# A graph layer with attention over edges, one core: the value product one step later, GpSimd waiting on ScalarE's counts, three PSUM banks each in the first phase, the scatters after the last record gather

## The chip, the core and the metric

One core of one Trainium2 chip runs the whole program. The metric is the device time of one execution in microseconds (us), lower is better. Below, PE is TensorE, DVE is VectorE, ACT is ScalarE, POOL is GpSimd and SP is SyncE.

## The reference

There are 100,000 nodes with 128 features each and 25,000 edges with a sender `snd` and a receiver `rcv`; the kernel sorts them by receiver. In the kernel's words:

```
score = silu(silu([x[rcv], x[snd], attr3, weight1] @ W1 + b1) @ W2 + b2) @ W3 + b3     one number an edge
alpha = softmax of score over the edges of one receiver
out[rcv] += alpha * node_vec[snd] * (x[snd] @ Wv)
result = layernorm(x + (x + out)) over the 128 features, all 100,000 rows
```

So every row of x is normalized at least as it is (the dense part), and the rows of receivers are written a second time with their sum (the edge part).

## The kernel before

**Groups and blocks.** The edges are padded to G = 49 groups of 512 (four tiles of 128). The dense part is 49 blocks of 2048 rows: SP loads a block (L306), DVE takes its statistics (L905, eight instructions), ACT and DVE normalize it in place (L477, 13 rows of 16; L920, the other three), SP stores it (L314). `dense_plan()` gives each block a turn: 17 of them in the first phase, one in three turns, the rest from the first step of the second phase on, eight in nine steps.

**First phase, 52 turns.** For each group in the senders' order: POOL gathers the sender's rows into the record ring (`hs`, L415, four indirect DMAs a group), PE transposes them (L583, bank i % 2), ACT copies the transpose to SBUF (L487, `hsT`, a ring of two), PE multiplies by the sender's part of W1 and adds the product of the edge attributes (L576 and L577, bank 2 + j % 4), ACT copies this into the record (L492), and SP writes the record to DRAM (L344). DVE sorts the edges by receiver meanwhile. PE's order in a turn i is: products of group i - 2, then the transposes of group i.

**Second phase, 66 steps.** It goes through the groups in the receivers' order. A group passes through these instructions, in the steps named (s is the step, g the group):

- POOL: gather of the receivers' rows (`hk`, L415, ten groups ahead), gather of the records (`r`, L415, ring of 12 groups), both four indirect DMAs a group
- PE, step g - 1: transposes of the receivers' rows (L596, `turn_rows`); ACT, step g: their copy (L500)
- PE, step g + 1: first layer, the product (L629) and the record added by four transposes (L631), which give `mm1_done`; ACT: first Silu (L510, `x1_ready`)
- PE, step g + 2: second layer (L623, `mm2_done`); ACT: second Silu (L505, `x2_ready`)
- PE, step g + 3: score (L616). Every four groups make a batch; DVE takes the batch's softmax in two parts (L943 to L953 and L959 to L964) with ACT's Exp (L515) between them
- PE, step g + 9: the receivers' numbers spread along rows (L606, `krow_ready`); DVE: the weight matrix (L973, `weights(g)`, `m_ready`)
- PE, step g + 10: the weighted sum of senders' rows (L645, `z_ready`); ACT: its copy `zs` (L520, `zs_ready`); PE, at the end of the same step: the product with Wv (L654, `y_ready`)
- DVE, step g + 11: the sum with the receiver's row (L982, `rows(g)`, `y_done`) and its statistics (L987); ACT, five steps or more later: the normalization (L529, `res_ready`)
- POOL: scatter of the finished rows to the output (`sc`, L419, four indirect DMAs a group)

All engines run in the order in which their instructions are written; the waits are on counts. PE's order in a step is: L606 (first waiting for `m_ready` of the group before, since bank 4 is reused), L616, L623, L629 and L631, a small transpose every fourth step (L639), L645, L596, L654. DVE's order in a step is: L920 of the dense block, `rows(s - 11)`, every fourth step the first part of the softmax, the dense statistics L905, `weights(s - 9)`, the second part of the softmax; the short instructions that turn statistics into factors (L876 to L890) are put between them.

**POOL's order** is written by `pool_plan()`: all `hs`; ten `hk`; then `r` and `hk` in turn; when the `hk` are used up, `r` 39 to 48 and `sc` 0 to 9 in turn (`SC_FROM` works out to 39); then the scatters 10 to 48. What POOL waits for before a group: `hs` g for T_ready (PE's transposes of group g - 5), `hk` 0 to 9 for A_ready (PE's products), `r` g for mm2_done (PE's second layer of group g - 3) and z_ready (group g - 12), `sc` g from 8 on for z_ready of group g + 26 and each for res_ready. After the last scatter POOL issues two more small scatters (L423), for receivers whose edges span tiles.

## Time and profile before

| what | us |
|---|---|
| median of 3 runs, lowest, highest | 1186.98, 1179.71, 1191.53 |
| the profiled execution | 1186.11 |
| its span, first to last instruction | 1177.9 |
| POOL busy | 752.8 (64%) |
| PE, DVE, ACT busy | 635.3, 586.4, 523.2 |

The span is 8.2 us shorter than the profiled execution's own time, and that one is 0.9 us under the median. Busy time of POOL is the writing of descriptors for indirect DMAs, 784 of them for the groups in four kinds (186.5, 189.9, 185.5 and 188.7 us); the 0.30 us between two of them counts as idle.

### The profile page before, as it was taken

To read this page: it belongs to the slowest core of one execution; us is meant where nothing else is said; L and a number is where in the kernel's file an instruction comes from. 1 tells how busy PE (TensorE), PEld (TensorE's weight loads), DVE (VectorE), ACT (ScalarE), POOL (GpSimd) and SP (SyncE) were. 2 spreads that over 40 slices of the span, in tenths; PEclk is the share of its full clock that TensorE was granted. 3 is DMA by queue.
4 is the path that set the end of the run, shared out by engine and by line. 5 is a ranking of instruction groups with operands and counts; after the bars stand their busy time and mean duration, and the time that the engine had idled before them with its cause. 6 is when DMAs were issued, how large, how long until landed. Compare 5 with 4: busy or idle time off the path is not lost.

```text
span 1177.9 us, 11360 instructions
## 1 busy us (share of the span) xinstructions
PE 635.3 (54%) x2783; PEld 436.6 (37%) x2783; DVE 586.4 (50%) x2276; ACT 523.2 (44%) x1168; POOL 752.8 (64%) x790
## 2 busy tenths in 40 slices
PE   2388778869703445666755766665555636610000
PEld 1256555546401222444434544444344425610000
DVE  4587665564431544597657766853323135532000
ACT  0255354355522556567667858765334324340000
POOL 7566666666677565656646656664656665577775
PEclk9999999999999976787877777787778777655555
DMA  6388877879974486575747566742212211121111
GB/s 207 101 257 289 256 261 245 275 263 253 292 240 147 162 287 235 165 249 188 243 159 242 200 214 213 245 143 81 72 55 68 68 54 40 44 71 52 53 51 38
DMA packets 77913, 199.67 MB, mean 170 GB/s; under 512 B 18999, under 2 KB 49398, under 8 KB 65304
## 3 DMA queue, kind: packets, MB, share of 16 engines
q1 hardware_dynamic: 49560, 134.47, 32.0%
q0 software_dynamic: 28288, 64.48, 20.4%
q8 instruction: 23, 0.38, 0.1%
q14 instruction: 42, 0.34, 0.1%
HBM read 106.74 MB, written 92.26 MB: 169 GB/s over the span
## 4 chain that ended last, share of the span: by engine, by line
PE 22%; ACT 21%; issue 18%; another core or an unknown queue 18%; POOL 10%; DVE 7%; SPq 2%; DMA 2%; ACTq 0%; POOLq 0%; DVEq 0%
ACT xin L477 12%; POOL out_rows L419 10%; PE bank L576 8%; PE bank L583 3%; ACT hk L529 3%; PE bank L577 3%; PE bank L654 2%; DVE dst L905 2%; PE bank L616 2%; PE bank L623 1%; DMA xin<-in_x 1%; ACT x L510 1%; ACT zs L520 1%; ACT hkT L500 1%
## 5 line engine op out<-in xcount | busy, mean ns | idle before, releaser
L415 POOL DMA_INDIRECT region<-rec_d,id_t x196 | 186.5, 952 | 172.4 <-PE bank L623 53.0
L477 ACT ACTIVATE xin<-xin,drs 128x128 f32<-128x128 f32 x637 | 257.9, 484 | 52.9 <-issue 32.4
L415 POOL DMA_INDIRECT hk<-in_xw,snd_t x196 | 189.9, 969 | 102.6 <-issue 54.9
L419 POOL DMA_INDIRECT out_rows<-hk,sidx_t x196 | 188.7, 963 | 76.4 <-issue 57.8
L415 POOL DMA_INDIRECT hk<-in_x,kg_t x196 | 185.5, 946 | 66.1 <-issue 58.8
L654 PE MATMUL bank<-wvh,zs 128*128 128x128 f32 x392 | 86.5, 389 | 215.6 <-ACT zs L520 151.3
L576 PE MATMUL bank<-w1b,region 128*128 128x128 f32 x392 | 151.3, 489 | 66.3 <-issue 43.7
L905 DVE BATCH_NORM_STATS2 dst<-xin 128x6 f32<-128x256 f32 x392 | 137.6, 416 | 67.1 <-DMA xin<-in_x 50.1
L654 PEld LDWEIGHTS bank<-wvh,zs 128*128 128x128 f32 x392 | 73.4, 280 | 227.2 <-ACT zs L520 159.3
L576 PEld LDWEIGHTS bank<-w1b,region 128*128 128x128 f32 x392 | 99.1, 313 | 91.8 <-issue 56.0
L982 DVE TENSOR_TENSOR hk<-bank,hk 128x512 f32<-128x512 f32 x49 | 33.8, 689 | 185.0 <-PE bank L654 79.4
L616 PE MATMUL bank<-x,wz 128*16 128x128 f32 x392 | 79.3, 372 | 26.7 <-ACT x L505 15.9
L505 ACT ACTIVATE x<-bank,bcol 128x512 f32<-128x512 f32 x49 | 33.6, 686 | 129.4 <-remote 105.9
L487 ACT ACTIVATE region<-bank 128x512 f32<-128x512 f32 x49 | 28.9, 590 | 138.9 <-PE bank L583 61.3
L623 PE MATMUL bank<-x,w2s 128*128 128x512 f32 x98 | 72.0, 824 | 19.9 <-ACT x L510 19.3
L529 ACT ACTIVATE hk<-hk,ers 128x128 f32<-128x128 f32 x196 | 79.8, 483 | 4.6 <-issue 3.2
L973 DVE TENSOR_SCALAR m_q<-bank,kcol,acol 128x128 f32<-128x128 f32 x196 | 73.4, 403 | 2.4 <-remote 2.2
L629 PE MATMUL bank<-hkT,w1a 128*128 128x512 f32 x98 | 55.2, 647 | 20.3 <-DMA region<-rec_d,id_t 19.4
L616 PEld LDWEIGHTS bank<-x,wz 128*16 128x16 f32 x392 | 45.6, 127 | 50.2 <-issue 18.8
L583 PE MATMUL bank<-ident,hk 128*128 128x128 f32 x196 | 54.3, 432 | 16.0 <-DMA w<-hk 16.0
L645 PE MATMUL bank<-m_q,region 128*128 128x128 f32 x392 | 59.3, 297 | 1.7 <-issue 1.6
L510 ACT ACTIVATE x<-bank,bcol 128x512 f32<-128x512 f32 x49 | 33.2, 677 | 57.3 <-remote 34.7
(179 smaller groups left out, 913.0 us busy)
## 6 DMA issues: line engine op xcount, KB each, us to landing
xin<-in_x SPq DMA_DIRECT2D x49, 1024.0 KB
out_rows<-xin SPq DMA_DIRECT2D x49, 1024.0 KB
rec_d<-hk SPq DMA_DIRECT2D x49, 514.0 KB
hk<-in_xw,snd_t POOLq DMA_INDIRECT x196
hk<-in_x,kg_t POOLq DMA_INDIRECT x196
region<-rec_d,id_t POOLq DMA_INDIRECT x196
out_rows<-hk,sidx_t POOLq DMA_INDIRECT x196
ef_d<-hk SPq DMA_DIRECT2D x9, 196.0 KB
```

Source lines behind the costliest of these rows:

```text
L415: pool.indirect_dma_start(out=to, out_offset=None, in_=frm, in_offset=bass.IndirectOffsetOnAxis(ap=index, axis=0)).then_inc(done, 16)
L419: pool.indirect_dma_start(out=out, out_offset=bass.IndirectOffsetOnAxis(ap=index, axis=0), in_=frm, in_offset=None).then_inc(done, 16)
L477: ins = nc.scalar.activation(xin[:, j % X_RING, n, :], xin[:, j % X_RING, n, :], ACT.Identity, bias=drs[:, j % 2, 1, n:n + 1], scale=drs[: ...
L529: ins = nc.scalar.activation(hk[:, g, q, :], hk[:, g, q, :], ACT.Identity, scale=ers[:, b % 2, 0, n:n + 1], bias=ers[:, b % 2, 1, n:n + 1])
L576: pe.matmul(to, hsT[:, j % 2, q * P:(q + 1) * P], w1b[:], start=True, stop=False)
L583: ins = pe.transpose(bank[i % 2][:, q * P:(q + 1) * P], rec[:, i % HS_RING, q, H:2 * H], ident[:])
L616: ins = pe.matmul(bank[3][0:BT, 0:P], wz[:, BT - 1 - n:2 * BT - 1 - n], x2[:, q * P:(q + 1) * P], start=(n == 0), stop=(last and q == TPG ...
L623: pe.matmul(bank[2][:], w2s[:], x1[:], start=True, stop=True).then_inc(S["mm2_done"], 1)
L645: ins = pe.matmul(bank[5][:, q * P:(q + 1) * P], rr[:, g % R_RING, q, H:2 * H], m_q[:, g % 2, q, :], start=True, stop=True)
L654: ins = pe.matmul(bank[6][:, q * P:(q + 1) * P], zs[:, q * P:(q + 1) * P], wvh[:], start=True, stop=True)
L905: ins = vec.bn_stats(dst[:, n:n + 2, :].rearrange("p j w -> p (j w)"), xin[:, j % X_RING, n:n + 2, :].rearrange("p j h -> p h j"))
L973: ins = vec.tensor_scalar(m_q[:, g % 2, q, :], bank[4][:, q * P:(q + 1) * P], kcol[:, t:t + 1], acol[:, b % 2, n:n + 1], ALU.is_equal, ALU ...
```

## The change

1. PE's product with Wv (L654 before) leaves the end of step g + 10 and stands in step g + 11, behind the first layer's L631 and ahead of L639 and L645. DVE's `rows(g)` stays in step g + 11.
2. POOL waits for ACT's counts where it waited for PE's: `hsT_ready` for T_ready (one group further ahead), `rec_ready` for A_ready (one further ahead), `x2_ready` for mm2_done (distance unchanged), `zs_ready` for z_ready ahead of the scatters. The wait of `r` for z_ready, which frees the ring, stays.
3. In the first phase the transposes use three banks, their copies a ring of three, and the products three banks instead of four; the waits follow these numbers.
4. No scatter stands between the record gathers: `sc` 0 comes after `r` 48.

```
+HST_RING, T_BANKS, A_BANKS = 3, (0, 1, 5), (2, 3, 4)
-HS_AHEAD, HK_AHEAD, R_AHEAD = 5, 6, 3
+HS_AHEAD, HK_AHEAD, R_AHEAD = 6, 7, 3
...
-        elif sc < G and r >= min(SC_FROM, G):
+        elif sc < G and r == G:
...
-                    wait(pool, "T_ready", g - HS_AHEAD + 1)
+                    wait(pool, "hsT_ready", g - HS_AHEAD + 1)
...
-                        wait(pool, "A_ready", min(G, G - HK_AHEAD + g))
+                        wait(pool, "rec_ready", min(G, G - HK_AHEAD + g))
...
-                    wait(pool, "mm2_done", g - R_AHEAD + 1)
+                    wait(pool, "x2_ready", g - R_AHEAD + 1)
...
-                        wait(pool, "z_ready", min(G, g + SC_AHEAD))
+                        wait(pool, "zs_ready", min(G, g + SC_AHEAD))
...
-                    wait(act, "A_ready", j - 1)
-                    nc.scalar.activation(hsT[:, j % 2, :], bank[j % 2][:], ACT.Copy).then_inc(S["hsT_ready"], 1)
+                    wait(act, "A_ready", j - HST_RING + 1)
+                    nc.scalar.activation(hsT[:, j % HST_RING, :], bank[T_BANKS[j % 3]][:], ACT.Copy).then_inc(S["hsT_ready"], 1)
...
-                    wait(pe, "rec_ready", j - 3)
+                    wait(pe, "rec_ready", j - 2)
...
-                    wait(pe, "hsT_ready", i - 1)
+                    wait(pe, "hsT_ready", i - 2)
...
+                g = s - Z_LAG - 1
+                if 0 <= g < G:
+                    wait(pe, "zs_ready", g + 1)
+                    wait(pe, "y_done", g)
+                    for q in range(TPG):
+                        ins = pe.matmul(bank[6][:, q * P:(q + 1) * P], zs[:, q * P:(q + 1) * P], wvh[:], start=True, stop=True)
+                    ins.then_inc(S["y_ready"], 1)
...
-                if 0 <= g < G:
-                    wait(pe, "zs_ready", g + 1)
-                    wait(pe, "y_done", g)
-                    for q in range(TPG):
-                        ins = pe.matmul(bank[6][:, q * P:(q + 1) * P], zs[:, q * P:(q + 1) * P], wvh[:], start=True, stop=True)
-                    ins.then_inc(S["y_ready"], 1)
```

PE in a middle step of the second phase, before, from one second-layer product (L623) to the next step's L616:

```order
L623 MATMUL bank<-x,w2s 128x512 [waits x2_ready,x1_ready]
L629 MATMUL bank<-hkT,w1a 128x512 [waits x1_ready,r_in10,hkT_ready]
L631 MATMUL bank<-ident,region 128x128 x4
L645 MATMUL bank<-m_q,region 128x128 [waits zs_ready,m_ready]
L645 MATMUL bank<-m_q,region 128x128 x3
L596 MATMUL bank<-ident,hk 128x128 [waits hkT_ready,hk_in4]
L596 MATMUL bank<-ident,hk 128x128 x3
L654 MATMUL bank<-wvh,zs 128x128 [waits y_done,zs_ready]
L654 MATMUL bank<-wvh,zs 128x128 x3
L606 MATMUL bank<-ident,kcol 128x128 [waits m_ready]
L606 MATMUL bank<-ident,kcol 128x128 x3
```

The same place after the change (the lines are two lower up to the new place, L650 is the old L645, L637 the old L654):

```order
L621 MATMUL bank<-x,w2s 128x512 [waits x2_ready,x1_ready]
L627 MATMUL bank<-hkT,w1a 128x512 [waits x1_ready,r_in10,hkT_ready]
L629 MATMUL bank<-ident,region 128x128 x4
L637 MATMUL bank<-wvh,zs 128x128 [waits y_done,zs_ready]
L637 MATMUL bank<-wvh,zs 128x128 x3
L650 MATMUL bank<-m_q,region 128x128 [waits zs_ready,m_ready]
L650 MATMUL bank<-m_q,region 128x128 x3
L594 MATMUL bank<-ident,hk 128x128 [waits hkT_ready,hk_in4]
L594 MATMUL bank<-ident,hk 128x128 x3
L604 MATMUL bank<-ident,kcol 128x128 [waits m_ready]
L604 MATMUL bank<-ident,kcol 128x128 x3
```

The product with Wv no longer follows its own zs; it stands ahead of L650, with the group before.

POOL around the last record gathers, before (`region` is the record ring, `sidx_t` the rows to write):

```order
L419 DMA out_rows<-hk,sidx_t 125089x128 [waits res_ready,dense_written]
L419 DMA out_rows<-hk,sidx_t 125089x128 x3
L415 DMA region<-rec_d,id_t 128x257 [waits mm2_done,z_ready]
L415 DMA region<-rec_d,id_t 128x257 x3
L419 DMA out_rows<-hk,sidx_t 125089x128 [waits res_ready]
L419 DMA out_rows<-hk,sidx_t 125089x128 x3
L415 DMA region<-rec_d,id_t 128x257 [waits mm2_done,z_ready]
```

After the change, around the last record gather:

```order
L413 DMA region<-rec_d,id_t 128x257 [waits x2_ready,z_ready]
L413 DMA region<-rec_d,id_t 128x257 x3
L417 DMA out_rows<-hk,sidx_t 125089x128 [waits res_ready,dense_written]
L417 DMA out_rows<-hk,sidx_t 125089x128 x3
L417 DMA out_rows<-hk,sidx_t 125089x128 [waits res_ready]
L417 DMA out_rows<-hk,sidx_t 125089x128 x3
```

Ten scatter groups, 40 indirect DMAs, have moved from between the last ten record gathers to behind them.

## Rows read from the trace of the kernel before

**Rows 1.** Windows: second phase with dense blocks, without, last scatters; times in us

```profile
core 0: us, PE busy (x) PEld busy (x) DVE busy (x) ACT busy (x) POOL busy (x), PEclk, DMA share, GB/s
492.00:833.00 341.00, 214.76 (x1090) 151.34 (x1088) 230.53 (x885) 228.78 (x513) 204.83 (x216) 0.77 0.58 193
833.00:945.00 112.00, 66.18 (x362) 47.30 (x362) 34.35 (x109) 41.93 (x80) 70.03 (x73) 0.77 0.22 64
1042.00:1169.00 127.00, 1.60 (x6) 0.86 (x6) 13.82 (x56) 9.64 (x23) 96.46 (x101) 0.50 0.18 57
```

**Rows 2.** Timeline, POOL, steps 23 and 24: start us, length us, instruction [idle before]

```profile
644.62 0.94 POOL L415 DMA_INDIRECT region<-rec_d,id_t  x1 [2.38 <-PE bank L645]
...
649.61 0.94 POOL L415 DMA_INDIRECT hk<-in_x,kg_t  x1 [0.30 <-issue]
...
653.36 0.94 POOL L415 DMA_INDIRECT hk<-in_x,kg_t  x1 [0.30 <-issue]
656.90 0.94 POOL L415 DMA_INDIRECT region<-rec_d,id_t  x1 [2.60 <-PE bank L623]
```

**Rows 3.** Timeline, PE, one step of the second phase, at the lower clock

```profile
635.07 2.07 PE L654 MATMUL bank<-wvh,zs 128*128 128x128 f32 x8 [4.11 <-ACT zs L520]
636.94 0.63 PE L606 MATMUL bank<-ident,kcol 128*128 128x128 bf16 x4
637.50 1.89 PE L616 MATMUL bank<-x,wz 128*16 128x128 f32 x8
639.32 1.85 PE L623 MATMUL bank<-x,w2s 128*128 128x512 f32 x2
641.01 1.02 PE L629 MATMUL bank<-hkT,w1a 128*128 128x512 f32 x2
641.87 0.60 PE L631 MATMUL bank<-ident,region 128*128 128x128 f32 x4
642.31 1.06 PE L645 MATMUL bank<-m_q,region 128*128 128x128 f32 x8
643.20 0.60 PE L596 MATMUL bank<-ident,hk 128*128 128x128 f32 x4
```

**Rows 4.** Timeline, ACT, the same step

```profile
643.88 0.69 ACT L505 ACTIVATE x<-bank,bcol 128x512 f32<-128x512 f32 x1 [3.39 <-remote]
...
646.70 1.28 ACT L515 ACT_TABLE_LOAD   x1
...
648.21 0.57 ACT L520 ACTIVATE zs<-bank 128x512 f32<-128x512 f32 x1
```

**Rows 5.** Timeline, DVE, from rows (L982) to the weights (L973), three steps

```profile
637.18 0.69 DVE L982 TENSOR_TENSOR hk<-bank,hk 128x512 f32<-128x512 f32 x1 [3.49 <-PE bank L654]
...
645.54 0.41 DVE L973 TENSOR_SCALAR m_q<-bank,kcol,acol 128x128 f32<-128x128 f32 x1
...
652.82 0.69 DVE L982 TENSOR_TENSOR hk<-bank,hk 128x512 f32<-128x512 f32 x1
...
658.03 0.41 DVE L973 TENSOR_SCALAR m_q<-bank,kcol,acol 128x128 f32<-128x128 f32 x1
...
856.07 0.69 DVE L982 TENSOR_TENSOR hk<-bank,hk 128x512 f32<-128x512 f32 x1 [8.38 <-remote]
...
857.47 1.35 DVE L973 TENSOR_SCALAR m_q<-bank,kcol,acol 128x128 f32<-128x128 f32 x4
```

**Rows 6.** Timeline, POOL: first phase, every third group of sender gathers

```profile
184.47 0.94 POOL L415 DMA_INDIRECT hk<-in_xw,snd_t  x1 [2.81 <-PE bank L583]
...
202.03 0.94 POOL L415 DMA_INDIRECT hk<-in_xw,snd_t  x1 [2.84 <-PE bank L583]
```

**Rows 7.** Timeline, POOL: record gather 39, record gather 48, a stall, last group scatter

```profile
833.17 0.94 POOL L415 DMA_INDIRECT region<-rec_d,id_t  x1 [2.73 <-PE bank L645]
...
944.55 0.99 POOL L415 DMA_INDIRECT region<-rec_d,id_t  x1 [3.73 <-PE bank L645]
...
973.21 0.95 POOL L419 DMA_INDIRECT out_rows<-hk,sidx_t  x1 [3.67 <-remote]
...
1167.57 0.95 POOL L419 DMA_INDIRECT out_rows<-hk,sidx_t  x1 [0.30 <-issue]
```

More of the change, by code:

```diff
@@ L89 @@
 DSTEP = dense_plan()
-SC_FROM = DSTEP[-1] - B0 + 5
 def pool_plan():
@@ L182, in part @@
             return region[:, at[0] - size:at[0]]
-        hsT = part(2 * GE).rearrange("p (r e) -> p r e", r=2)
+        hsT = part(HST_RING * GE).rearrange("p (r e) -> p r e", r=HST_RING)
         ef = part(EF_RING * GE // 2).bitcast(BF16).rearrange("p (r e) -> p r e", r=EF_RING)
@@ L491, in _ @@
                     wait(act, "A_ready", j + 1)
-                    nc.scalar.activation(rec[:, j % HS_RING, :, 0:H], bank[2 + j % 4][:].rearrange("p (q h) -> p q h", q=TPG), ACT.Copy
+                    nc.scalar.activation(rec[:, j % HS_RING, :, 0:H], bank[A_BANKS[j % 3]][:].rearrange("p (q h) -> p q h", q=TPG), ACT.Copy
                                          ).then_inc(S["rec_ready"], 1)
@@ L572, in _ @@
                     wait_ring(pe, ef_in, j, 16)
-                    wait(pe, "rec_ready", j - 3)
+                    wait(pe, "rec_ready", j - 2)
                     for q in range(TPG):
-                        to = bank[2 + j % 4][:, q * P:(q + 1) * P]
-                        pe.matmul(to, hsT[:, j % 2, q * P:(q + 1) * P], w1b[:], start=True, stop=False)
+                        to = bank[A_BANKS[j % 3]][:, q * P:(q + 1) * P]
+                        pe.matmul(to, hsT[:, j % HST_RING, q * P:(q + 1) * P], w1b[:], start=True, stop=False)
                         ins = pe.matmul(to, ef[0:36, j % EF_RING, q * P:(q + 1) * P], w36[:], start=False, stop=True)
@@ L580, in _ @@
                     wait_ring(pe, hs_in, i, 16 * TPG)
-                    wait(pe, "hsT_ready", i - 1)
+                    wait(pe, "hsT_ready", i - 2)
                     for q in range(TPG):
-                        ins = pe.transpose(bank[i % 2][:, q * P:(q + 1) * P], rec[:, i % HS_RING, q, H:2 * H], ident[:])
+                        ins = pe.transpose(bank[T_BANKS[i % 3]][:, q * P:(q + 1) * P], rec[:, i % HS_RING, q, H:2 * H], ident[:])
                     ins.then_inc(S["T_ready"], 1)
```

## The prediction

> **What bounds the kernel now.** I read the busy shares first: no engine is near full, POOL is highest at 64%. So I cut the span into stages (windows) and looked in each for the engine whose instructions stand in a row with the same gap at the same place.
>
> At the end it is POOL. The last scatter starts at 1167.57 and nothing but the two small ones and the landing comes after it: 1168.5 to 1177.9, 9.4 us [rows 7]. Between 1042 and 1169 us POOL issues 101 indirect DMAs in 127 us, 1.26 us each, of which 0.96 is work and 0.30 the step to the next [rows 1]; that is 5.05 us a group of four, and no wait is left there. So the end is the moment at which POOL may begin its uninterrupted scatters plus their number times 5.05 us. Record gather 48 is issued at 944.55 and takes 5.05, so it is done at 949.6; 39 scatter groups follow up to 1168.5, 218.9 us, against 39 x 5.05 = 197.0 without a stall. 22 us are waits for the last sums, one of which is seen ending at 973.21 [rows 7].
>
> In the middle, 492 to 833 us, there is a step of 12.2 to 12.3 us. POOL shows it: a record gather at 644.62, eight indirect DMAs until 654.30, idle for 2.60 us, the next record gather at 656.90 [rows 2]; 10.0 of work and 2.3 of waiting for PE's count. PE shows its own loop: the Wv product waits 4.11 us for ACT's zs [rows 3], and behind it come L606, L616, L623, whose result ACT's second Silu reads, and after more of ACT's work the next zs at 648.21 [rows 4]. Both loops have the same length, so either may lead. One thing counts for what follows: by its row L623 ends at 641.17, yet ACT and POOL, both waiting for it, start at 643.88 and 644.62 [rows 2 to 4]. PE's counts arrive up to 2.7 us behind the ends in its rows, and there POOL had gone idle (at 642.24) shortly before. The Trainium skill, "Perfetto Trace Analysis", section "Tensor Engine Instruction (MATMUL, LD_WEIGHTS)", says that TensorE's end is an estimate from the size and that the count follows the acknowledgement of PSUM; it gives no size for the delay. The trace agrees that there is one.
>
> In the first phase POOL issues three sender groups, 15.0 us, and then waits 2.84 us: 17.56 us from 184.47 to 202.03, 5.85 us a group [rows 6].
>
> **The change, part by part, against the profiled execution (span 1177.9 us, 8.2 us around it, 0.9 us below the median).**
>
> *First phase: 0 us, bounds -33 and +10.* POOL's wait for T_ready of group g - 5 becomes one for the copy of group g - 6. The copy follows its transposes at once or, where ACT is in a block of 13 norms, behind that block; the extra group ahead is 5 us of POOL. I let them cancel. The third bank for the transposes frees nothing by itself: in PE's order the products of group i - 2, which wait for that group's copy, stand ahead of the transposes of group i, so the old wait was already met. If the gap of 2.5 us went in each third group of 39, it would be 13 x 2.5 = -33; if each became 0.7 longer, +10. I take 0: the loop of copy, products and transposes between PE and ACT is untouched.
>
> *Second phase, record gathers wait for x2_ready: +0.7 us a step.* The group is the same, so the wait can only end later, by one Silu, 0.69 us [rows 4]; in the step behind an Exp also by a table load, 1.28 us [rows 4]. POOL's loop becomes 12.3 + 0.7 = 13.0 us, every fourth step 14.3. Behind the waiting gather stand the four gathers of receivers' rows, ten groups ahead, which nobody lacks.
>
> *Wv product a step later: the zs wait goes, and a tighter loop comes.* The 4.11 us wait of PE [rows 3] is gone, since zs of the group before is long there. What is late next is m_ready. Before, DVE's rows(g) used a product made a step earlier; now the product of group g is made in the same step g + 11, in the middle of PE's list. DVE does rows, statistics and the weights in this order, and L606 at the head of PE's next step waits for these weights. So each step has the loop: L606 to the Wv product on PE, rows to weights on DVE. PE's part at the lower clock: 636.94 to 642.31 for L606 to L631, 5.4 us, plus 2.07 for the product, 7.5 us [rows 3]. DVE's part: 652.82 to 658.44, 5.6 us; in the fourth step with the softmax 637.18 to 645.95, 8.8 us [rows 5]. With 0.1 for the handing over: 13.2 us, and 16.4 in every fourth step. The granted clock of the stage is 0.77 [rows 1], that is about half the time at 2.4 instead of 1.2 GHz, which takes some 2 us off PE's part in such steps; then POOL's 13.0 leads. Four steps together: 13.1, 13.1, 14.3 and 15.0, mean 13.9 against 12.2. That is +1.7; I take +1.6: the stage's 27 steps have 341 us, 12.6 each [rows 1], so some are longer than 12.3 by other causes and should absorb theirs. Bounds: 0 a step (DVE's part finds room that I don't see) and +2.8 (all at the lower clock and PE's counts late as well).
> Steps 12 to 38, 27 of them: 27 x 1.6 = +43 us. Steps 3 to 11 have only the x2 part: 9 x 0.7 = +6 us.
>
> *Record gathers 39 to 48 without scatters between them: -20 us.* Now nine steps take 944.55 - 833.17 = 111.4 us, 12.4 each [rows 7], though there is no dense block left and POOL has 10 us of work in each. Then POOL has 5 us, and the PE and DVE loop leads: DVE's part is 856.07 to 858.82, 2.8 us [rows 5], PE's at most 7.5, so 10.3 us, one in four longer by the softmax, some shorter at the higher clock. I take 10.2: 9 x 2.2 = 20. Bounds: 0 and -40 (8 us a step, the clock at 2.4 GHz).
>
> *Scatters: ten groups move to the end.* What stands after gather 48 is 49 x 5.05 = 247.5 us instead of 197.0, +50.5 us, on the path in full. The 22 us of waits in that stretch were waits for sums of the last groups; twelve groups that need none of them now come first, so most is covered. I keep 5, bounds 0 and 25. zs_ready for z_ready adds 0.6 us at a hold and is within this.
> The Trainium skill, "Perfetto Trace Analysis", section "Optimization Strategy", says that where the most-contended engine changes over time, interleaving the regimes may help. This part undoes such an interleaving. By the rule alone the price is the 50.5 us; by the rows the scatters were not free where they stood, and 20 come back.
>
> *Sum.* Gather 48 is issued at 944.6 + 0 + 6 + 43 - 20 = 973.6; + 5.05 + 247.5 + 5 + 9.4 = 1240.5 us of span; + 8.2 + 0.9 = 1249.6. I round to 1249 us, 5% more than 1187.
>
> **The rivals.**
> *Only the scatters count.* The new loop costs nothing, POOL's Silu wait is hidden, the last nine steps give 20: gather 48 at 924.6, span 1191.5, time 1201 us. For it: DVE has only 230.5 us of work in the 341 of the stage [rows 1]. Against it: the order is fixed, and DVE idles for the product, not for lack of work. Chance 0.20, half of it within 1% of now.
> *Faster: POOL's gap closes.* With the zs wait gone PE's second layer could be done while POOL is still issuing, so that gather g never waits: a step is POOL's 10.0 us. 27 x 2.3 = 62 us and 20 in the last steps put gather 48 at 862.6, span 1129.5, time 1139 us. It needs m_ready to come early, which rows 5 speak against. It decides from where gather 48 is issued before 917: 917 + 5.05 + 247.5 + 9.4 is today's 1178 of span. Chance 0.12.
> *Slower still: late counts on top.* PE's counts are late while POOL issues without a pause (the 3.67 us stall at 973.21 follows 25 us of such issuing [rows 7]), and now DVE's rows wait for one of them in the middle of the step. A step of 15.0 in steps 12 to 38 gives 27 x 2.8 = 76, ten more in the first phase, 20 more of holds: 1249 + 33 + 10 + 20 = 1312 us at the end, 1290 as its middle. Chance 0.16.
>
> **How the numbers follow.** The forecast has 0.52. The likeliest alone spans 1225 to 1275 (step +0.8 to +2.6 and the holds). For 8 in 10 the range goes down to the scatters-only case and up into the late-counts one: 1195 to 1292. About 1% is what a measurement of this kernel tells from no change. Slower by over 1%: 0.52 + 0.16 + 0.10 from the scatters-only case + 0.01 = 0.79. Within 1%: 0.08 of that case. Faster: 0.12, and 0.01 of rest.
>
> **What would show it.** In the timeline of the changed kernel: PE no longer waits for ACT's zs, and its first L604 of a step waits for DVE's m_q; DVE's L982 waits for the Wv product in each step and L973 ends some 5.6 us later; POOL's gap before a record gather is 3 us or more, released by ACT; gather 48 between 950 and 1000; then 49 scatter groups of 5.05 us with almost no gap. I am wrong if the steps between 492 us and the end of the dense blocks stay at 12.3 us or less, if gather 48 comes before 925, or if the scatters don't end the program.

## The result, and the profile after

The changed kernel takes 1274.06 us (median of 4 runs, 1270.66 to 1278.11) beside 1187.75 us (4 runs) for the kernel before: 1.077 times as long, 95% interval 1.072 to 1.082. The forecast was 1249 with a range of 1195 to 1292. The profiled execution of the changed kernel took 1270.66 us, its span 1262.5.

The same stages as in [rows 1], cut where the changed kernel has them (record gathers 12 to 38, 39 to 47, then two pieces of the scatters):

```profile
core 0: us, PE busy (x) PEld busy (x) DVE busy (x) ACT busy (x) POOL busy (x), PEclk, DMA share, GB/s
501.00:899.00 398.00, 219.79 (x1087) 141.92 (x1087) 227.12 (x876) 228.76 (x509) 204.12 (x216) 0.73 0.50 168
899.00:974.00 75.00, 58.69 (x342) 39.77 (x343) 34.70 (x113) 40.53 (x77) 33.98 (x36) 0.89 0.24 65
979.00:1122.00 143.00, 56.62 (x277) 44.63 (x277) 44.24 (x143) 30.83 (x68) 88.55 (x94) 0.62 0.13 44
1128.00:1253.00 125.00, 1.60 (x6) 0.86 (x6) 12.34 (x49) 7.88 (x19) 95.09 (x99) 0.50 0.18 57
```

Every engine does the work that it did, in a longer stage: VectorE 227 us where it had 231, ScalarE the same 229, GpSimd the same 204. The time is waiting. By the starts of the record gathers and the end of the span the 84.6 us of more span lie so:

| stretch | before | after | difference | the prediction had |
|---|---|---|---|---|
| start to record gather 0 | 349.6 | 356.8 | +7 | 0 |
| record gathers 0 to 12 | 142.6 | 144.1 | +1.5 | +6 |
| 12 to 39 | 341 | 398 | +57 | +43 |
| 39 to 48 | 111.4 | 75 | -36 | -20 |
| gather 48 to the end | 233.4 | 288.1 | +55 | +33.5 (50.5 and 5, less the 22 of waits) |

The costliest groups of the page (busy and mean, then the idle time before them and what ended it):

```profile
L413 POOL DMA_INDIRECT region<-rec_d,id_t x196 | 185.2, 945 | 242.4 <-ACT x L503 155.9
L413 POOL DMA_INDIRECT hk<-in_xw,snd_t x196 | 187.8, 958 | 112.0 <-issue 57.9
L981 DVE TENSOR_TENSOR hk<-bank,hk 128x512 f32<-128x512 f32 x49 | 33.9, 691 | 288.0 <-remote 152.3
L604 PE MATMUL bank<-ident,kcol 128*128 128x128 bf16 x196 | 26.0, 275 | 238.6 <-DVE m_q L972 176.5
```

GpSimd now waits for ScalarE's second Silu (L503), and TensorE for VectorE's weights. Of the 288.0 us that VectorE stands before its rows (L981), the profile puts 128.2 down to the product with Wv (L637) and 152.3 to nobody ("remote"). The wait of 4.11 us for zs at the head of the product [rows 3] is nearly gone: all such waits together are 10.5 us, where they were 151.3. One step of the changed kernel, in the place of [rows 3 and 5]; TensorE first, then VectorE:

```profile
755.33 0.60 PE L604 MATMUL bank<-ident,kcol 128*128 128x128 bf16 x4 [10.43 <-issue]
755.86 1.89 PE L614 MATMUL bank<-x,wz 128*16 128x128 f32 x8
757.68 2.08 PE L621 MATMUL bank<-x,w2s 128*128 128x512 f32 x2
759.55 1.91 PE L627 MATMUL bank<-hkT,w1a 128*128 128x512 f32 x2
761.77 1.06 PE L637 MATMUL bank<-wvh,zs 128*128 128x128 f32 x8
...
768.55 0.61 PE L604 MATMUL bank<-ident,kcol 128*128 128x128 bf16 x4 [4.04 <-DVE m_q L972]
```

```profile
762.86 0.69 DVE L981 TENSOR_TENSOR hk<-bank,hk 128x512 f32<-128x512 f32 x1 [2.38 <-PE bank L637]
...
764.27 2.72 DVE L904 BATCH_NORM_STATS2 dst<-xin 128x6 f32<-128x256 f32 x8
...
768.09 0.41 DVE L972 TENSOR_SCALAR m_q<-bank,kcol,acol 128x128 f32<-128x128 f32 x1
```

This is the loop of the prediction: 7.5 us from L604 to the end of L637, then rows, eight statistics and the weights, 5.6 us, then L604 again: 13.2 us. TensorE's granted clock is 0.50, the lower level, up to 761 us and 1.00, the higher, from 761.7 on, so L637's matmuls (1.06 us, where they took 2.07 in [rows 3]) already ran at the higher one. Behind it stand the second layer (L621) and so the Silu for which GpSimd waits.

The other half of the story is two steps earlier in the same trace. GpSimd, TensorE, VectorE and ScalarE:

```profile
700.82 0.95 POOL L413 DMA_INDIRECT region<-rec_d,id_t  x1 [9.78 <-ACT x L503]
...
719.56 0.94 POOL L413 DMA_INDIRECT hk<-in_x,kg_t  x1 [0.30 <-issue]
735.09 0.94 POOL L413 DMA_INDIRECT region<-rec_d,id_t  x1 [14.59 <-ACT x L503]
```

```profile
710.58 1.06 PE L637 MATMUL bank<-wvh,zs 128*128 128x128 f32 x8
...
729.17 0.61 PE L604 MATMUL bank<-ident,kcol 128*128 128x128 bf16 x4 [16.21 <-DVE m_q L972]
```

```profile
723.28 0.69 DVE L981 TENSOR_TENSOR hk<-bank,hk 128x512 f32<-128x512 f32 x1 [16.33 <-remote]
```

```profile
723.37 0.60 ACT L518 ACTIVATE zs<-bank 128x512 f32<-128x512 f32 x1 [7.79 <-remote]
```

The rows of the product end at 711.64. VectorE, which waits for nothing else, starts at 723.28, 11.6 us later. GpSimd had issued sixteen indirect DMAs in a row from 700.82 to 720.50; 2.8 us after it fell idle VectorE and ScalarE both got their counts within 0.1 us. This step took 25 us. "remote" is what the profile writes where it finds nobody who could have released the wait at that time; this trace lacks over a third of the records of VectorE's counts, more than a quarter of ScalarE's and a sixth of TensorE's, which makes the word frequent here.

### The profile page after: what moved, and what is told of

It is laid out like the page before. It is cut to its first block, busy times and chain, and to the rows that moved or that the text cites. A ratio compares the mean times of both kernels' runs of the same rounds, so it can differ in the third digit from the quotient of the medians.

```text
span 1262.5 us, 11358 instructions
## 1 busy us (share of the span) xinstructions
PE 638.4 (51%) x2783; PEld 425.1 (34%) x2783; DVE 584.6 (46%) x2276; ACT 526.2 (42%) x1168; POOL 748.4 (59%) x790
## 4 chain that ended last, share of the span: by engine, by line
DVE 22%; another core or an unknown queue 22%; PE 21%; issue 16%; ACT 9%; POOL 8%; DMA 2%; SPq 0%; POOLq 0%; DVEq 0%; ACTq 0%
POOL out_rows L417 8%; ACT xin L475 6%; DVE dst L904 5%; PE bank L621 4%; PE bank L614 4%; DVE m_q L972 3%; PE bank L637 3%; PE bank L627 3%; PE bank L574 2%; DVE hk L981 2%; DMA xin<-in_x 2%; DVE est L986 1%; PE bank L604 1%; DVE cwd L883 1%
## 5 line engine op out<-in xcount | busy, mean ns | idle before, releaser
L413 POOL DMA_INDIRECT region<-rec_d,id_t x196 | 185.2, 945 | 242.4 <-ACT x L503 155.9
L981 DVE TENSOR_TENSOR hk<-bank,hk 128x512 f32<-128x512 f32 x49 | 33.9, 691 | 288.0 <-remote 152.3
L604 PE MATMUL bank<-ident,kcol 128*128 128x128 bf16 x196 | 26.0, 275 | 238.6 <-DVE m_q L972 176.5
L604 PEld LDWEIGHTS bank<-ident,kcol 128*128 128x128 bf16 x196 | 15.2, 119 | 250.7 <-DVE m_q L972 185.8
L621 PE MATMUL bank<-x,w2s 128*128 128x512 f32 x98 | 87.7, 992 | 11.3 <-ACT x L508 11.1
L627 PE MATMUL bank<-hkT,w1a 128*128 128x512 f32 x98 | 68.2, 787 | 35.1 <-DMA region<-rec_d,id_t 25.6
L503 ACT ACTIVATE x<-bank,bcol 128x512 f32<-128x512 f32 x49 | 33.5, 684 | 115.5 <-remote 74.3
L518 ACT ACTIVATE zs<-bank 128x512 f32<-128x512 f32 x49 | 28.8, 588 | 123.3 <-remote 92.3
L637 PE MATMUL bank<-wvh,zs 128*128 128x128 f32 x392 | 59.0, 299 | 21.2 <-issue 16.2
L650 PE MATMUL bank<-m_q,region 128*128 128x128 f32 x392 | 62.4, 304 | 13.7 <-issue 13.7
```

The lines of the kernel that those rows point to most:

```text
L413: pool.indirect_dma_start(out=to, out_offset=None, in_=frm, in_offset=bass.IndirectOffsetOnAxis(ap=index, axis=0)).then_inc(done, 16)
L621: pe.matmul(bank[2][:], w2s[:], x1[:], start=True, stop=True).then_inc(S["mm2_done"], 1)
L627: pe.matmul(bank[1][:], w1a[:], hkT[:, g % 2, :], start=True, stop=False, skip_group_check=True)
L637: ins = pe.matmul(bank[6][:, q * P:(q + 1) * P], zs[:, q * P:(q + 1) * P], wvh[:], start=True, stop=True)
L650: ins = pe.matmul(bank[5][:, q * P:(q + 1) * P], rr[:, g % R_RING, q, H:2 * H], m_q[:, g % 2, q, :], start=True, stop=True)
```

## The experiments

"Chip A" below is where the kernel before takes 1188 us; "prompt" chips took 997 us for the same program. The record numbers the chip of e1 to e4 (15) and the prompt ones (10, 6 and 14), not that of the first measurement, and no chip was measured in both conditions. So whether it is the chip or a condition that it was in is open, and "chip A" stands for either. The expectations of e10 to e13 call it the late one. In each table "gather n" is the start of record gather n, and "step" the mean over gathers 12 to 39.

### On chip A: the change taken apart

**e1_product_later_alone**, the kernel before with the product moved and nothing else:

```diff
                     ins.then_inc(S["mm1_done"], 1)
+                g = s - Z_LAG - 1
+                if 0 <= g < G:
+                    wait(pe, "zs_ready", g + 1)
...
                 if s + 1 < G:
                     turn_rows(s + 1)
-                if 0 <= g < G:
-                    wait(pe, "zs_ready", g + 1)
...
```

> Before, with only the Wv product moved behind the first layer of the next step. Loop theory (product, DVE's rows, weights, PE's next L606 in one step): nearly the whole price of the steps, so steps 12 to 38 take 14 to 14.7 us instead of 12.6, record gather 39 comes 40 to 60 us later than in before (833), the end 30 to 60 us later: ratio 1.03 to 1.05, and L606 waits for DVE's weights by over 100 us in all. Rival theory (POOL's wait for x2_ready makes the steps long): the move alone is neutral or gains its 4 us of zs wait, ratio 0.98 to 1.01.

**e2_scatters_behind_alone**:

```diff
-        elif sc < G and r >= min(SC_FROM, G):
+        elif sc < G and r == G:
```

> Before, with only the ten scatter groups moved behind the last record gather. Scatter theory: gather 48 comes 20 to 36 us earlier than 944.6, 50.5 us of scatters stand behind it, and the last sums are late because PE's counts are late while POOL issues without a pause, so POOL waits 20 to 45 us there: ratio 1.02 to 1.045. Rival (the scatters were free where they stood, nothing comes back): ratio 1.045 or more with gather 48 at 940 to 950. Rival (waits in the tail are covered by the twelve free groups): ratio 1.01 to 1.02, under 6 us of waits.

**e3_counts_alone**, the counts for which GpSimd waits, with their distances; no third banks:

```diff
-HS_AHEAD, HK_AHEAD, R_AHEAD = 5, 6, 3
+HS_AHEAD, HK_AHEAD, R_AHEAD = 6, 7, 3
...
-                    wait(pool, "T_ready", g - HS_AHEAD + 1)
+                    wait(pool, "hsT_ready", g - HS_AHEAD + 1)
...
-                        wait(pool, "A_ready", min(G, G - HK_AHEAD + g))
+                        wait(pool, "rec_ready", min(G, G - HK_AHEAD + g))
...
-                    wait(pool, "mm2_done", g - R_AHEAD + 1)
+                    wait(pool, "x2_ready", g - R_AHEAD + 1)
...
-                        wait(pool, "z_ready", min(G, g + SC_AHEAD))
+                        wait(pool, "zs_ready", min(G, g + SC_AHEAD))
```

> Before, with only POOL's waits on ScalarE's counts and their distances. Loop theory: +0.7 us a step at most (one Silu), partly hidden; ratio 1.00 to 1.02, gather 39 at 833 to 860. Rival (the counts of ScalarE are what makes the steps long): gather 39 at 870 to 900, ratio 1.03 to 1.06. First phase: the last sender gather within 8 us of before's 288.

**e4_rows_also_later**, the changed kernel with VectorE's rows a step later as well, first in its step, so that the loop product, rows, weights no longer closes within one step:

```diff
-Y_LAG, Z_LAG, M_LAG = 11, 10, 9
+Y_LAG, Z_LAG, M_LAG = 12, 10, 9
...
+                if 0 <= s - Y_LAG < G:
+                    rows(s - Y_LAG)
...
-                if 0 <= s - Y_LAG < G:
-                    rows(s - Y_LAG)
```

> The changed kernel, with DVE's rows(g) also a step later (step g + 12, first in its step), so that the product has a step of slack again as it had before. Loop theory: PE's wait for DVE's weights goes, steps 12 to 38 take 12 to 13 us, gather 39 at 835 to 860, the time falls by 40 to 60 us against the changed kernel: ratio against before 1.02 to 1.045, what is left being the scatters. Rival (x2_ready, or late counts of PE whatever the loop): steps stay over 14 us, ratio 1.06 to 1.08.

| chip A | ratio, 95% interval | gather 0 | step | gathers 39 to 48 | gather 48 |
|---|---|---|---|---|---|
| before | 1 | 350 | 12.6 | 111 | 945 |
| e1, product | 1.029 (1.022 to 1.036) | 351 | 13.6 | 112 | 977 |
| e2, scatters | 1.001 (0.997 to 1.004) | 352 | 12.5 | 61 | 892 |
| e3, counts | 1.050 (1.044 to 1.056) | 364 | 13.8 | 114 | 997 |
| e4, changed with rows later | 1.062 (1.056 to 1.068) | 363 | 14.7 | 65 | 969 |
| changed | 1.077 (1.072 to 1.082) | 357 | 14.8 | 75 | 974 |

*e1* came near what the loop theory had, and a little under it: ratio 1.029 for 1.03 to 1.05, steps of 13.6 us for 14 to 14.7, gather 39 31 us later for 40 to 60. L606 waits 123 us in all for VectorE's weights, as that theory asked (over 100).

*e2* missed my 1.02 to 1.045: the scatters were not dear but even, within the interval. Gather 48 comes 52 us earlier, the 50.5 us of scatters come after it, and the last sum is copied when it was.

*e3* missed by the most: I had 1.00 to 1.02, and it is the dearest part. Fourteen us of it lie in the first phase, 32 in steps 12 to 38, and those are not one Silu in each step: four of 27 steps are 21 to 22 us long. One of them, GpSimd first, then ScalarE:

```profile
537.48 0.95 POOL L415 DMA_INDIRECT region<-rec_d,id_t  x1 [3.21 <-ACT x L505]
...
547.50 0.95 POOL L415 DMA_INDIRECT region<-rec_d,id_t  x1 [0.30 <-issue]
...
568.68 0.95 POOL L415 DMA_INDIRECT region<-rec_d,id_t  x1 [11.40 <-ACT x L505]
```

```profile
545.45 0.69 ACT L505 ACTIVATE x<-bank,bcol 128x512 f32<-128x512 f32 x1 [2.21 <-issue]
...
557.51 0.69 ACT L510 ACTIVATE x<-bank,bcol 128x512 f32<-128x512 f32 x1 [9.83 <-remote]
```

The x2 of 545.45 was in time for once, so GpSimd went on to the next gather without a pause and issued for 20 us in a row. TensorE's first-layer rows end at 545.67, and ScalarE's Silu of them starts at 557.51, 0.2 us after GpSimd's last issue ended at 557.28. In each of the four long steps the step before it had taken 10 us, that is, its gather had followed without a pause, and in each a count of TensorE came over 11 us late. In the kernel before only two steps are over 16 us, and they look the same.

*e4* missed as well (I had 1.02 to 1.045; its rival, 1.06 to 1.08, holds): with the loop undone by order the step stays 14.7, now 13 steps of 10 us and 11 of over 16. In each of these eleven some of TensorE's counts came over 12 us late. So on this chip GpSimd runs on where the loop no longer stops it, and the late counts are found behind such stretches. In *e1*, whose own long steps (four, 16.9 to 17.6 us) are those with the softmax, no count in them is over 3 us late.

The parts come to 36.6 (e1) + 59.8 (e3) + 1.0 (e2) = 97 us, the change as a whole, which has the third banks too, to 86 us. The third banks were not tried alone, and no worth of theirs shows: the first phase of e4 is that of the changed kernel, banks and all, and costs 13 us in its trace, where the changed kernel's costs 7 and e3's, without the banks, 14.

### On other chips: the same parts without late counts

The next kernels were meant to split e3. The chip they ran on took 996.65 us for the kernel before, and two further chips took nearly the same (996.86 and 996.92).

**e7_before_rows_gather_one_more**, and once more as **e13_before_rows_gather_one_more_again**: the kernel before with

```diff
-HS_AHEAD, HK_AHEAD, R_AHEAD = 5, 6, 3
+HS_AHEAD, HK_AHEAD, R_AHEAD = 5, 6, 4
```

> The kernel before with one number changed: the record gathers may run four groups ahead of the second layer's product instead of three, so GpSimd is released a step earlier. Theory 'just in time' (in the kernel before each gather starts some 1.7 us after GpSimd falls idle, because the count it waits for comes only then, and this sets the 12.2 to 12.6 us step): with one more group of lead GpSimd finds its count there, the steps of groups 12 to 38 go down towards its own 10.0 us, gather 39 begins near 780 us instead of 833, and the time is 0.95 to 0.98 of before. Rival 'late counts' (TensorE's counts come late as long as GpSimd issues without a pause): GpSimd issues two or three groups in a row, TensorE then stands until it pauses, steps come in pairs of about 10 and 20 us, gather 39 stays between 825 and 890, and the time is 0.99 to 1.05 of before.

> The same kernel as e7 (the kernel before, record gathers released four groups ahead instead of three). On a prompt chip 1.000 again. On the late chip, theory 'TensorE's counts stay away while GpSimd issues without a pause': GpSimd's gathers come two or more groups in a row, TensorE stands for 8 us or more after each such run, steps 12 to 38 mean 12.4 to 14 us with some over 18, ratio 0.995 to 1.05. Rival 'just in time' (the wait of some 2.4 us ahead of each record gather is what sets the step): steps of 10 to 11.5 us and a ratio of 0.95 to 0.98.

**e8_second_phase_wait_alone** (before, one line), and **e9_first_phase_waits_alone** (before, e3's new distances and its two waits of the first phase):

```diff
-                    wait(pool, "mm2_done", g - R_AHEAD + 1)
+                    wait(pool, "x2_ready", g - R_AHEAD + 1)
```

> The kernel before with only the wait of the record gathers changed: for ScalarE's count of the second layer's Silu (x2) in place of TensorE's count of the product, same distance of three; first phase, product with Wv and scatters as before. Theory 'the 5% of the counts lie in the second phase, as two gathers in a row followed by a step of some 20 us': first phase within 3 us of before, steps of groups 12 to 38 mean 13.6 to 14.0 with three to six of them over 18 us, ratio 1.03 to 1.045. Rival 'it is one Silu a step': all steps 0.5 to 1.0 us longer and none over 16, ratio 1.01 to 1.025. Rival 'it was the first phase that shifted the rest': this run is within 1% of before.

> The kernel before with only the two waits of the first phase changed (source gathers for ScalarE's count of the transposed copy at a distance of 6, the second gathers for the record count at 7); banks, record gathers, product and scatters as before. Theory 'the first phase costs its own 14 us and the second is untouched': record gather 0 begins at 360 to 366 us instead of 350, steps 12 to 38 stay 12.4 to 12.8, ratio 1.008 to 1.015. Rival 'no cost': record gather 0 within 4 us of 350 and ratio 0.997 to 1.004. Rival 'it also turns the second phase over': ratio over 1.02.

**e5_no_scatter_before_last_sum**, and again on another prompt chip as **e11_no_scatter_before_last_sum_again**: the changed kernel with

```diff
-SC_HOLD, SC_AHEAD = 8, 26
+SC_HOLD, SC_AHEAD = 0, 49
```

> The changed kernel with no scatter issued before the copy of the last group's sum, so that GpSimd stands idle from the last record gather (some 980 us) until then; nothing else is changed. Theory 'TensorE's counts come late while GpSimd issues': the last sum's copy comes 80 to 95 us after the start of gather 48 (changed kernel 146, kernel before 91), no wait of ScalarE or VectorE on a TensorE count over 4 us in the steps after 48; all 49 groups of scatters then run in one piece of 245 to 250 us, and the span is 1305 to 1325 us. Rival 'the last ten steps are long by their own chain (product, rows, weights)': the last sum's copy still comes 125 to 150 us after the start of gather 48 and the span is 1350 us or more.

> The same kernel as e5 (the changed kernel with no scatter issued before the copy of the last sum). Theory 'TensorE's counts come late while GpSimd issues, on the late chip alone': on the late chip the last sum's copy comes 70 to 90 us after the start of gather 48 where the changed kernel took 146, since GpSimd stands idle there; on the prompt chip it comes 71 us after it as in e5. Rival 'on the late chip they are late whatever GpSimd does': 120 us or more on the late chip.

**e10_product_back**, the changed kernel with e1's edit turned round (counts, banks and scatters stay), and **e12_changed_again**, the changed kernel unaltered:

> The changed kernel with the product with Wv put back to the end of its step; the three banks, GpSimd's waits on ScalarE's counts and the scatters behind the last records stay as changed. Two chips have been seen: one (call it the late one, 1187.8 us for the kernel before) on which TensorE's counts arrive up to 20 us after its rows, and one (the prompt one, 996.6 us) on which they come with the rows and GpSimd issues from the first instruction to the last. Theory 'two causes' (the loop product, rows, weights costs 2 us a step on both chips; the waits on ScalarE's counts cost only where TensorE's counts are late): on the prompt chip this kernel is 0.998 to 1.005 of before with steps 12 to 38 of 10.0 us, on the late one 1.04 to 1.065 with steps of 13.4 to 14.2. Rival 'the parts hold each other up': on the prompt chip over 1.02, on the late one over 1.065 or under 1.03.

> The changed kernel, once more and unaltered, beside the kernel before on whichever chip comes. Theory 'the loop product, rows, weights is a cost of its own on any chip': on a prompt chip (kernel before 997 us) first phase and the gathers up to 12 as before, steps 12 to 38 of 12.0 to 12.6 us against 10.0 as in e5, gather 48 near 833 us, last sum's copy 905 to 925, ratio 1.085 to 1.11; on the late chip (1188 us) 1.072 to 1.082 as first measured. Rival 'the change costs only where TensorE's counts are late': 0.99 to 1.02 on a prompt chip.

| prompt chips | ratio, 95% interval | step | gathers 39 to 48 | gather 48 | last sum copied |
|---|---|---|---|---|---|
| e7, e13 (4 ahead) | 1.000 (0.999 to 1.001) | 10.0 | 91 | 784 | 841 |
| e8, x2 wait | 1.000 (0.999 to 1.001) | 10.0 | 92 | 784 | 844 |
| e9, first phase | 1.000 (0.999 to 1.001) | 10.0 | 91 | 783 | 839 |
| e10, product back | 1.008 (1.007 to 1.010) | 10.0 | 56 | 748 | 808 |
| e12, changed | 1.095 (1.092 to 1.097) | 12.6 | 70 | 831 | 902 |
| e5, e11 | 1158 to 1159 us, one run each | 12.7 | 70 | 833 | 904 |

*e7, e8, e9, e13* say nothing about e3 on chip A, for which they were made: on these chips GpSimd never waits, so no count for which it waits can cost anything. The page of e8 shows all four kinds of its groups with nothing before them but the 0.3 us from one instruction to the next (196 x 0.30 = 59 us; the first kind has the 2.6 us of the start as well):

```profile
L415 POOL DMA_INDIRECT hk<-in_xw,snd_t x196 | 189.2, 965 | 62.0 <-issue 58.5
L419 POOL DMA_INDIRECT out_rows<-hk,sidx_t x196 | 188.5, 962 | 59.8 <-issue 59.2
L415 POOL DMA_INDIRECT region<-rec_d,id_t x196 | 186.0, 949 | 59.7 <-issue 58.5
L415 POOL DMA_INDIRECT hk<-in_x,kg_t x196 | 185.7, 947 | 59.7 <-issue 58.2
```

On these chips e7, e8, e9 and e13 are one uninterrupted train of 784 indirect DMAs and the two small ones, and their 997 us are that train. The kernel before takes the same time there; no trace of it was kept, so that it is the same train is inferred. The third of these lines in the kernel before on chip A:

```profile
L415 POOL DMA_INDIRECT region<-rec_d,id_t x196 | 186.5, 952 | 172.4 <-PE bank L623 53.0
```

*e10 and e12* separate the product from the rest. Without its move the change costs 9 us (1005.74 against 996.86), with it 94 (1090.70 against 996.92). So 85 us are the product, on chips where GpSimd left no gap to hide it. e10 is a small miss (I had 0.998 to 1.005): with the scatters gone from between them the last record gathers wait, 70.5 us before all of them where e8 has 59.7. e12 came as forecast, but for the last sum's copy, 3 us early. The windows of e13 (equal to before in time), then of e12, gathers 12 to 38, 39 to 47, and the rest of GpSimd's train:

```profile
422.00:693.00 271.00, 196.60 (x1092) 136.17 (x1090) 220.26 (x856) 223.81 (x503) 205.18 (x217) 0.88 0.69 239
693.00:784.00 91.00, 68.15 (x362) 47.17 (x362) 38.76 (x125) 43.17 (x82) 69.06 (x73) 0.85 0.27 79
784.00:991.00 207.00, 41.76 (x246) 33.96 (x244) 54.73 (x188) 37.35 (x86) 157.29 (x164) 0.58 0.18 57
```

```profile
421.00:760.00 339.00, 213.62 (x1085) 138.68 (x1083) 220.56 (x848) 228.26 (x505) 203.97 (x216) 0.78 0.57 191
760.00:831.00 71.00, 56.28 (x338) 38.72 (x338) 33.05 (x106) 38.61 (x72) 34.55 (x38) 0.93 0.26 69
836.00:1084.00 248.00, 47.83 (x279) 38.49 (x277) 60.60 (x209) 41.65 (x93) 188.27 (x197) 0.58 0.17 56
```

The first lines: 271 us against 339, at equal work of VectorE, +68. The granted clock falls from 0.88 to 0.78 in the stretch in which TensorE now stands for VectorE's weights, and its rows take 17 us more for the same matmuls. So part of the loop's price seems to come from the lower clock and not from the order. In a step that begins at the lower clock TensorE's 7.5 us and VectorE's 5.7 close as on chip A; the count comes at once here. Two L604 and what lies between:

```profile
441.96 0.61 PE L604 MATMUL bank<-ident,kcol 128*128 128x128 bf16 x4 [4.61 <-DVE m_q L972]
...
448.37 1.06 PE L637 MATMUL bank<-wvh,zs 128*128 128x128 f32 x8
...
455.16 0.61 PE L604 MATMUL bank<-ident,kcol 128*128 128x128 bf16 x4 [4.40 <-DVE m_q L972]
```

```profile
449.47 0.69 DVE L981 TENSOR_TENSOR hk<-bank,hk 128x512 f32<-128x512 f32 x1 [4.65 <-PE bank L637]
```

13.2 us from L604 to L604, and L637's end at 449.43 releases VectorE at 449.47: 0.04 us, where chip A had 11.6 in the step shown above.

*e5 and e11*, whose first expectation (80 to 95 us, span 1305 to 1325) was made for chip A: with GpSimd idle after gather 48 the last sum's copy comes 71 us after that gather begins; in e12, with GpSimd scattering all the while, also 71. So on prompt chips GpSimd's issuing costs the other engines nothing there. On chip A the changed kernel takes 146 for the same ten steps. The kernel that was to show whether an idle GpSimd brings chip A's counts back never ran on chip A.

No version beat the kernel before, on chip A or on the prompt ones. On the prompt ones none can that has the same 784 indirect DMAs without a faster way to issue them.

## Why the prediction was right, and where it was not

The sign, the place of the end (an uninterrupted train of scatters, gather 48 at 974.4 where 973.6 stood) and the mechanism of the largest term held. The sum was 22 us short of the profiled span (1240.5 against 1262.5). That it came so near is in part luck: three terms were too small, by 7, 14 and 21 us, and two stretches came out shorter than I had them, by 5 and 16. Up to gather 48 these misses cancel, which is why it came at the forecast time.

*First phase, 0 us (bounds -33 and +10).* +7 on chip A, and +14 in e3. "The extra group ahead is 5 us of POOL. I let them cancel" failed. ScalarE's count follows one of TensorE's, which comes late there; that this is the whole reason is argued, not shown. On a prompt chip the waits are free (e9: 1.000).

*Record gathers wait for x2_ready, +0.7 us a step.* The term was mis-sized, and its reason incomplete. "The wait can only end later, by one Silu" holds for one step. What it left out is that a step in which x2 happens to be in time lets GpSimd run 20 us without a pause, and that TensorE's counts came over 11 us late behind such a stretch. e3 has +32 us over 27 steps, 1.2 a step, and four long steps where the kernel before has two. In gathers 0 to 12 the change took +1.5 us, where this term had +6. How much of e3 is this wait alone, on chip A, stays open.

*Product a step later, the loop.* Right in mechanism and near in size for the plain step: 13.1 predicted, 13.2 in both traces shown. That TensorE's part is 7.5 us in each is luck. The prediction read [rows 3] as the lower clock throughout, but the granted clock there is 0.50 up to 639 us and 1.00 from 641 on. So it added a first-layer product mostly at the higher clock (1.02 us) and a product at the lower (2.07), and the changed kernel has them the other way round (L627 1.91, L637 1.06). e10 against e12 shows it alone, +85 us; e1 on chip A +37, which I put down to the steps having been 12.6 already there. I had given this loop and GpSimd's Silu wait together +1.6 a step; they made +2.1 (57 us in 27 steps). The softmax's price was too small: in the steps that have it the loop is 17 to 18 us also on a prompt chip (four of 27), where I had 16.4 at the lower clock and 15.0 in the sum. Of the nine steps of the changed kernel over 16 us on chip A, five are such and have no count over 3 us late. The other four, the one of 25 us shown above among them, have counts 11 to 15 us late.

*Gathers 39 to 48, -20 us (bounds 0 and -40).* -36. The term was mis-sized: it took "PE's at most 7.5" nearly in full. The granted clock there rose from 0.77 to 0.89, TensorE's part, from L604 to the end of L637, is 4.6 us in five of nine steps and 6.2 to 6.5 in four, and the steps are 8.4 us instead of my 10.2. In e2, without the loop, the clock is 1.00 and the steps 6.7.

*Scatters, +50.5 us and 5 of waits (bounds 0 and 25).* The 50.5 is right to the us (e10, e12: 247.3 and 247.8 us for the train on prompt chips, 247.5 worked out). The waits are 26 on chip A, one past the bound: 979.4 to 1253.0 is 273.7, less 247.5. "Twelve groups that need none of them now come first, so most is covered" failed. While GpSimd issues these groups without a pause, the sums do not come:

```profile
1009.90 2.08 PE L621 MATMUL bank<-x,w2s 128*128 128x512 f32 x2
...
1013.48 0.85 PE L629 MATMUL bank<-ident,region 128*128 128x128 f32 x4
1029.88 2.07 PE L637 MATMUL bank<-wvh,zs 128*128 128x128 f32 x8 [15.56 <-issue]
```

```profile
1029.23 0.60 ACT L518 ACTIVATE zs<-bank 128x512 f32<-128x512 f32 x1 [37.09 <-remote]
...
1058.64 0.69 ACT L503 ACTIVATE x<-bank,bcol 128x512 f32<-128x512 f32 x1 [27.27 <-remote]
```

```profile
1048.82 0.95 POOL L417 DMA_INDIRECT out_rows<-hk,sidx_t  x1 [0.30 <-issue]
1060.66 0.96 POOL L417 DMA_INDIRECT out_rows<-hk,sidx_t  x1 [10.89 <-ACT zs L518]
```

From 979.4 to 1049.8 GpSimd issues fourteen groups. The second Silu (L503) reads what L621 left at 1011.98 and starts at 1058.64, 46.7 us later. In these 70 us the other engines get through little more than one step, which takes 8 us before and after. Then GpSimd falls idle for 10.89 us and everything moves again. By itself the move is even on chip A (e2), and it costs 0.8% on prompt chips with the counts and banks beside it (e10).

*The rivals.* "Only the scatters count" fell with e1 and e10. "POOL's gap closes" fell: GpSimd's idle time before record gathers rose from 172.4 to 242.4 us. What it describes, a step of GpSimd's own 10.0, exists, but on the prompt chips, in every run without the product's move (e7 to e10, e13). "Late counts on top" is the rival to which the result leans in part: its mechanism is in the trace in four long steps and in the tail. Its 1312 us were too much, since steps 12 to 38 took 57 us more and not 76, and gathers 39 to 48 gave back 36 and not 20. I had it at 0.16. In e3, which has no loop, it goes with a larger price (60 us) than the loop alone in e1 (37), so it should have had a term of its own in the sum. In the changed kernel the two are mixed: in steps 12 to 38 fewer counts are over 1 us late (58 of the 178 recorded) than in the kernel before (102 of 172).

*The rule on interleaving* (the Trainium skill, "Perfetto Trace Analysis", section "Optimization Strategy"), which spoke against moving the scatters: e2 shows a price of 0.1% within an interval 0.7% wide, and what standing alone costs, its faster steps (6.7 us) give back.

## What to carry to other kernels

Before you move a product into the same step as the work that uses it, write down the loop that this closes within one step: one engine's part, its count, the other engine's part. If that is longer than the step, the loop is the new step, whatever wait was removed; here 7.5 + 5.6 us against 10.0 to 12.6. A wait that a profile shows on one chip may be that chip's: what a kernel's structure allows is read from the engine's own train of work (784 times 1.25 us here), and an edit that shortens such a wait should be tried on a chip that has it and on one that has not. Where an engine waits in every step, ask also what happens in the step in which it need not: on chip A GpSimd then issued for 20 us in a row, and the counts that the others waited for came late.

## What the hardware showed that I had not expected

The same program takes 1188 us on chip A and 997 on three others (996.65 to 996.92, in agreement to 0.03%). GpSimd's instructions are equally long on both (945 to 969 ns). What differs is when others see that TensorE is done: 0.04 us after the end of its rows on a prompt chip, on chip A 2.7 us in a plain step [rows 3, 4], 11.6 us after sixteen indirect DMAs issued without a pause, and 46.7 us under the fourteen groups of scatters. In the steps shown of e3 and of the changed kernel a count came 0.2 and 2.8 us after GpSimd fell idle, in the tail 8.9 us after it; but others came while it was still issuing (the zs at 1029.23), so the pause is not a strict condition.

The traces hold more on this than single steps. I set each recorded count of TensorE beside the last end before it of the rows that raise it, which gives the least delay that it can have. On the prompt chips none of some 450 in a run is over 0.1 us late. In the kernel before on chip A 203 of 363 are over 1 us late, and 146 of these come 1.5 to 3.5 us after GpSimd fell idle; in the changed kernel 134 of 365 and 69. ScalarE's recorded counts are within 0.1 us of its rows in both of these and on the prompt chips. Chip A's traces also lack many records of counts (12% to 17% of TensorE's, 28% to 42% of ScalarE's), the prompt ones next to none; what that has to do with the delay is not known.

TensorE's row ends are worked out by the profile, so whether its matmuls or its counts are held is not to be told from these traces. That the cause is GpSimd's issuing is what most of these rows agree with, and what no kernel here has shown by itself on chip A.

The Trainium skill, "Perfetto Trace Analysis", section "Tensor Engine Instruction (MATMUL, LD_WEIGHTS)", has the count follow the acknowledgement of PSUM. The prompt chips' traces agree, with 0.04 us from the end of the rows to the engine that waits; for chip A's 2.7 to 46.7 us it names nothing that would take longer.
